# A three-layer graph attention stack on one core: own products in the first sixteen blocks, one running maximum instead of two and a join, extremes one count tile later

## The reference

```python
h = x @ W
s, d = h @ a_src, h @ a_dst
e = leaky_relu(s[src] + d[dst], 0.2)
m = segment_max(e, dst)
ex = exp(e - m[dst])
alpha = ex / segment_sum(ex, dst)
out = segment_sum(alpha[:, None] * h[src], dst) + b
```

## Time and profile before

| | us |
|---|---|
| median of 3 runs (lowest, highest) | 688.24 (688.14, 689.72) |
| the profiled execution | 687.7 |
| its span | 686.0 |
| busy: PE / DVE / ACT / POOL | 587.9 / 639.8 / 484.7 / 459.6 |

### The profile page before, as it was taken

The page is one execution under the profiler, slowest core; times in us unless marked ns, Lnnn a source line. Parts: engine busy times, 40 slices in busy tenths (PEclk is TensorE's granted clock), DMA queues, the critical chain, the costliest instruction groups (busy, mean ns, idle before and its releaser), DMA issues.

```text
span 686.0 us, 13824 instructions
## 1 busy us (share of the span) xinstructions
PE 587.9 (86%) x5571; PEld 570.1 (83%) x5571; DVE 639.8 (93%) x911; ACT 484.7 (71%) x719; POOL 459.6 (67%) x448
## 2 busy tenths in 40 slices
PE   1728845989869899999999979999989989999995
PEld 1628744988769899989999979899989979999994
DVE  3999979999999989999987999999998899999994
ACT  0416543655969787887765878989886698898891
POOL 5579103589908656675954775858598688697883
PEclk9959977899999899999999999999999999999998
DMA  2410002000000000000100100000010010110001
GB/s 69 119 56 2 1 9 38 1 2 1 20 1 1 20 1 20 1 1 9 20 20 1 27 1 20 1 19 2 8 20 20 1 27 3 37 29 11 20 1 42
DMA packets 22325, 12.07 MB, mean 18 GB/s; under 512 B 12393, under 2 KB 20055, under 8 KB 22255
## 3 DMA queue, kind: packets, MB, share of 16 engines
q1 hardware_dynamic: 21455, 9.85, 6.2%
q0 software_dynamic: 800, 1.26, 0.6%
HBM read 9.47 MB, written 1.64 MB: 16 GB/s over the span
## 4 chain that ended last, share of the span: by engine, by line
DVE 52%; PE 28%; issue 8%; DMA 6%; POOL 4%; ACT 1%; POOLq 0%; DVEq 0%; SPq 0%
PE ps L1813 21%; DVE scratch L951 21%; DVE ps L1067 16%; DVE scratch L1149 5%; DMA xr<-in_x 3%; POOL scratch L751 2%; DVE ps L1069 2%; DVE ps L1079 1%; PE ps L1866 1%; PE ps L1821 1%; DMA gathered<-ext_lines 1%; PE ps L1844 1%; DVE scratch L1067 1%; DMA gathered<-in_edges,start_i 1%; DMA ext_lines<-ext 1%
## 5 line engine op out<-in xcount | busy, mean ns | idle before, releaser
L1813 PE MATMUL ps<-hB,scratch 125*125 125x129 f32 x3450 | 404.7, 276 | 21.3 <-DVE scratch L1149 17.8
L1813 PEld LDWEIGHTS ps<-hB,scratch 125*125 125x125 f32 x3450 | 390.7, 189 | 28.6 <-DVE scratch L1149 23.0
L751 POOL TENSOR_TENSOR scratch<-scratch,C 125x625 f32<-125x625 f32 x239 | 304.1, 1283 | 124.1 <-ACT scratch L1569 122.1
L1067 DVE SCALAR_TENSOR_TENSOR ps<-C,a_unit,ps 125x625 f32<-125x625 fp8e3 x330 | 275.5, 867 | 2.3
L1567 ACT ACTIVATE scratch<-gathered,r_neg 125x625 f32<-125x625 f32 x219 | 176.6, 806 | 18.7 <-PE ps L1813 17.5
L1569 ACT ACTIVATE scratch<-scratch,r_src 125x625 f32<-125x625 f32 x219 | 179.0, 817 | 7.1
L1452 ACT ACTIVATE C<-ps 125x1000 fp8e3<-125x1000 f32 x80 | 78.0, 1000 | 78.5 <-PE ps L1780 78.3
L1780 PE MATMUL ps<-scratch 128*128 128x125 bf16 x1250 | 90.3, 235 | 40.0 <-DVE scratch L951 38.1
L1780 PEld LDWEIGHTS ps<-scratch 128*128 128x128 bf16 x1250 | 83.0, 105 | 46.8 <-DVE scratch L951 44.7
L1149 DVE SCALAR_TENSOR_TENSOR scratch<-ps,r_src,C 125x625 f32<-125x625 f32 x121 | 104.2, 861 | 4.2 <-PE ps L1803 4.1
L951 DVE TENSOR_TENSOR scratch<-key_lo,ps 128x4096 bf16<-128x4096 bf16 (+3 forms) x41 | 89.8, 2190 | 0.0
(11 more groups left out here) (195 smaller groups left out, 451.5 us busy)
## 6 DMA issues: line engine op xcount, KB each, us to landing
gathered<-g_lines SPq DMA_DIRECT2D x15, 305.2 KB
xr<-in_x SPq DMA_DIRECT2D x1, 1562.5 KB
out<-xr SPq DMA_DIRECT2D x4, 312.5 KB
edge_sb<-in_edges SPq DMA_DIRECT2D x1, 805.7 KB
gathered<-ext_lines SPq DMA_DIRECT2D x5, 122.1 KB
w<-in_W SPq DMA_DIRECT2D x2, 128.0 KB
out<-xr SPq DMA_DIRECT2D x1, 187.5 KB
out<-xr SPq DMA_DIRECT2D x1, 125.0 KB
```

Of the source, the lines that this page charges most:

```text
L751: g.tensor_tensor(slot[s], slot[s], C5[:, q % NC, s, :], ALU.mult).then_inc(pool_done, 1)
L1067: v.scalar_tensor_tensor(dest, counts, unit[:, s:s + 1], top, ALU.min, ALU.max).then_inc(S.top_done, 1)
L1813: last = mm(ps[0:P, acc_at(t):acc_at(t) + HW], A[:, P * t:P * (t + 1)], feat, start=opens and t in (0, 3), stop=closes, skip_group_check=True)
```

## The change

- One accumulator `TOP0` for all tops of a chunk; the join goes, and every top waits for the top before it. Top 24 writes `top_a`.
- Other tables of own products. The number per chunk stays (4, 9, 7, 11, then 12, 10, 10, 10, 10, 12, 9, 9, 9, 9). Chunks 6 to 9 have 0, 1, 2, 4, 6, 8, 10, 12, 14 and 16 (20 and 24 have become 6 and 12), chunks 11 to 14 have 1, 2, 4, 6, 8, 10, 12, 14 and 16 in the same manner. Chunks 5 and 10 keep theirs.
- The next row of G comes two blocks behind the last own product: after block 21, 19 and 19 in chunks 1 to 3, after 18 in chunks 6 to 8 and 11 to 13. Chunks 4 and 9 keep 22, chunks 5 and 10 keep 23. Its wait for the tops goes.
- The extremes are taken at count tile 15 instead of 14 and reduced two tiles later (17) instead of one (15). Chunk 0's blocks then lie in tiles 22 to 35.

```diff
-        OWN = ((), (15, 18, 20, 22), (1, 4, 7, 10, 13, 15, 18, 20, 22), (1, 5, 9, 13, 16, 19, 22), (0, 2, 4, 7, 10, 12, 14, 16, 18, 20, 22))
+        OWN = ((), (13, 15, 17, 19), (0, 2, 4, 7, 9, 11, 13, 15, 17), (1, 3, 5, 8, 11, 14, 17), (0, 2, 4, 6, 8, 10, 12, 14, 15, 16, 18))
...
-        EXT_AT = FEAT_AT[-1] + 2
-        OVER_AT = EXT_AT + 1
+        EXT_AT = FEAT_AT[-1] + 3
+        OVER_AT = EXT_AT + 2
...
-        MORE = (0, 6, 12, 18, 22)
+        INNER = ((0, 1, 2, 4, 6, 8, 10, 12, 14, 16), (1, 2, 4, 6, 8, 10, 12, 14, 16))
...
-            if q < NC:
-                return ODD
             if turn(q):
                 return tuple(sorted(ODD + TURN_MORE))
-            return tuple(sorted(ODD + MORE[(1 if q < 2 * NC else 0):]))
+            return tuple(s for s in range(T) if s not in INNER[q // NC - 1])
...
         def rows_at(q):
-            return 23 if turn(q) else 22
+            return 22 if q % NC == NC - 1 else min(23, max(s for s in range(T) if s not in POOL_OF[q]) + 2)
...
-                odd = in_odd(s, q if S is F else None)
-                at_ = TOP1 if odd else TOP0
-                top = ps[0:P, at_:at_ + CD]
-                same = [k for k in range(s) if in_odd(k, q if S is F else None) == odd]
-                if same:
-                    dve.wait_ge(S.top_done, n + same[-1] + 1)
-                elif q:
+                n = q * T + s
+                top = ps[0:P, TOP0:TOP0 + CD]
+                if n:
                     dve.wait_ge(S.top_done, n)
...
-            def join_tops(S, q):
-                dve.wait_ge(S.top_done, q * (T + 1) + T)
-                v.tensor_tensor(top_a, top_a, ps[0:P, TOP0:TOP0 + CD], ALU.max).then_inc(S.top_done, 1)
...
                 for t in range(CT):
-                    if t == CT - 1 and q > 1:
-                        pe.wait_ge(F.top_done, tops_before_rows(q))
```

More of the change, by code:

```diff
@@ L441, in post_at @@
             return TURN[L] if turn(q) else BEFORE_LAST[L] if q % NC == NC - 1 and L < 2 else USUAL[L]
-        def in_odd(k, q=None):
-            if q in (1, 2):
-                return k % 2 == 1 and not any(at_ == AFTER and (c, k) == (q, k_) for at_, c, k_ in FIRST_TOPS[q])
-            return k >= AHEAD and k % 2 == 1
-        LAST_ODD = max(k for k in range(T) if in_odd(k))
-        def tops_before_rows(q):
-            if q in (2, 3):
-                c, k = min((c, k) for at_, c, k in FIRST_TOPS[q - 1] if at_ == AFTER)
-                return c * (T + 1) + k
-            return q * (T + 1) if q > 1 else 0
         def top_at(q, k):
@@ L459, in top_at @@
             return (k - AHEAD) * (T - 3) // (T - 1 - AHEAD)
-        def join_at(q):
-            return top_at(q, T - 1) if turn(q) else top_at(q, T - 1) + 1
         def rows_at(q):
-            return 23 if turn(q) else 22
+            return 22 if q % NC == NC - 1 else min(23, max(s for s in range(T) if s not in POOL_OF[q]) + 2)
         def pool_no(q, s):
@@ L1053, in top_step @@
                 counts = C5[:, q % NC, s, :]
-                n = q * (T + 1)
-                odd = in_odd(s, q if S is F else None)
-                at_ = TOP1 if odd else TOP0
-                top = ps[0:P, at_:at_ + CD]
-                same = [k for k in range(s) if in_odd(k, q if S is F else None) == odd]
-                if same:
-                    dve.wait_ge(S.top_done, n + same[-1] + 1)
-                elif q:
+                n = q * T + s
+                top = ps[0:P, TOP0:TOP0 + CD]
+                if n:
                     dve.wait_ge(S.top_done, n)
-                if s == LAST_ODD and q:
+                if s == T - 1 and q:
                     dve.wait_ge(S.top_T, q)
-                dest = top_a if s == LAST_ODD else top
-                if same:
+                dest = top_a if s == T - 1 else top
+                if s:
                     v.scalar_tensor_tensor(dest, counts, unit[:, s:s + 1], top, ALU.min, ALU.max).then_inc(S.top_done, 1)
@@ L1162, in first_tops @@
                         next_top(c, k)
-                        if k == T - 1:
-                            join_tops(F, c)
             def chunk(q):
@@ L1178, in chunk @@
                                 next_top(q, k)
-                        if s == join_at(q):
-                            join_tops(F, q)
                     if q:
@@ L1371, in careful_chunk @@
                     top_step(K, a_unit[0], q, i)
-                join_tops(K, q)
                 for part in range(3):
@@ L1784, in top_transpose @@
             def top_transpose(S, q):
-                pe.wait_ge(S.top_done, (q + 1) * (T + 1))
+                pe.wait_ge(S.top_done, (q + 1) * T)
                 if q:
```

## The result

The changed kernel takes 703.85 us in the median (703.76 to 704.38), the kernel before beside it 688.19. The ratio is 1.0225, with a 95% interval of 1.0211 to 1.024: by it 15.5 us slower; the spans of the two profiles are 702.0 and 686.0. The forecast was 694.8 with a range of 687.5 to 700. The sign was right, the size was not.

The account below looks back on a forecast made before the run. VectorE and TensorE were taken to bound the kernel in turns: their loop in chunks 6 to 9, VectorE's sum in chunks 11 to 14. Terms summed to +6.5, 694.2 profiled, 694.8 us median; range 687.5 to 700.

Parts of the forecast that it names:

- Count stage, -3.4: Count stage: later extremes remove VectorE's 3.39 us wait for them, -3.4 us, bounds -3.4 and 0.
- The price of a chained pair and of a join: VectorE's tops: one following a top of the same accumulator costs 0.13 us more; a join costs 0.72 us.
- The rival of a free chain: VectorE's tops: chained tops cost nothing extra, so dropping joins gains and the time is 677.3 us; chance 0.13.
- Start of chunk 1, +3.5: Start of chunk 1: block 13's product now comes first, delaying block 15 and the reduction; +3.5 us, bounds 0 and 6.
- Chunks 2 to 4, +0.3: Chunks 2 to 4: more chained pairs, fewer joins, denser products, TensorE waiting elsewhere about as much; +0.3 us, bounds -0.5 and +2.
- Chunks 6 to 8, +4.8: Chunks 6 to 8: the TensorE-VectorE loop grows by 1.4 us and ScalarE adds 0.2, 1.6 a period; +4.8 us.
- Chunk 9, 0: Chunk 9: the same +1.4 us at block 14, offset by less waiting for GpSimd; 0, bounds -0.5 and +1.5.
- Chunks 11 to 13, +1.0: Chunks 11 to 14, three periods: VectorE's added work costs +0.3 us each; +1.0 us, bounds -1.5 and +3.
- VectorE's sum: Chunks 11 to 14: VectorE's total work, issued without a gap, sets the period; +1.04 - 0.72 = +0.3 us each.
- The end, +0.9: End of chunk 14: GpSimd's last block becomes 24, adding 1.28 less 0.4; +0.9 us, bounds 0 and +2.6.
- The row of G: Next row of G sooner, without its wait: VectorE waited only at the start of chunks 5 and 10; 0 us.
- The rival of eight GpSimd blocks in a row: Blocks 17 to 24, all GpSimd's: TensorE waits 1 us more in chunks 6 to 14, 7 more, 701.8; chance 0.15.

Follow-up runs that it names:

- e1: Kernel before with only the extremes taken one tile later and reduced two tiles later; 685.66 us, ratio 0.9953.
- e2: Kernel before with only one accumulator and no join, old product tables kept, row of G not waiting for the tops; 693.71 us, ratio 1.0073.
- e9: Kernel before with block 22 in place of block 8 as VectorE's product in chunks 6 to 9; 691.81 us, ratio 1.0034.
- e11: Kernel before with VectorE's blocks 6 and 12 for 20 and 24 in chunks 6 to 9 and 11 to 14; 698.32 us, ratio 1.0144.
- e5: Kernel before with the new tables of VectorE's own products in chunks 1 to 4 alone; 693.5 us, ratio 1.0076.
- e7: Kernel before with block 6 in place of block 20 for VectorE in chunks 6 to 9 and 11 to 14; 696.31 us, ratio 1.011.
- e8: Kernel before with block 12 in place of block 24 for VectorE in chunks 6 to 9 and 11 to 14; 690.31 us, ratio 1.0021.
- e4: Changed kernel with the next row of G back at block 22 or 23; 705.33 us, ratio 1.0229 to the kernel before.

## Why the prediction was right or wrong

The forecast was +6.5 on the profiled execution, the profile has +16.0. The terms that were too small are those of chunks 2 to 4 (by 2.3 us), the end (2.1), the start of chunk 1 (1.75), chunks 11 to 13 (1.3) and chunk 9 (1.1).

- **Count stage, -3.4.** Right: -3.6 in the table, -3.2 alone (e1).
- **The price of a chained pair and of a join.** Right: 0.912 against 0.775, and e2 costs 5.0 where the price gives 5.5. The rival of a free chain falls. So does the rule of the Trainium skill ("VectorE: DVE Perf Modes", section "The DRAIN you can't avoid") as applied to this pattern, where every top needs the one before.
- **Start of chunk 1, +3.5.** The mechanism was right (block 13's product ahead of two blocks and the transpose), the term too small: +5.25 in the table, 4.4 for the chunk's table of products alone. What failed is "I take the stretch at 1.2 GHz as falling half into it: -1.7". The idle time of 7.28 us ended with the clock already at the low level, and blocks 13 and 14 and the transpose ran wholly at it, 2.8 us more on the way to the reduction. In the kernel before the low clock cost about 1.1 at the reduction in chunk 2 (32.0 us from one reduction to the next, 30.9 in e9 and e11, which have no fall). That 3.5 + 1.7 comes to the measured 5.25 is in part luck: the stage differs by 1.1 between profiles of the same code.
- **Chunks 2 to 4, +0.3.** Wrong: +2.6, above the bound of 2. "VectorE's products come denser; TensorE waits at other blocks by about as much" left both costs out. The chain costs 2.1 here (e2), the tables 1.7 (e5). In the changed kernel +1.4 lie between the reductions in chunks 3 and 4, where e2 has +1.6 and e5 nothing, and +1.1 between those in chunks 4 and 5, where e5 has +1.15 and e2 nothing; there TensorE waits 0.57 for GpSimd and 0.26 for ScalarE.
- **Chunks 6 to 8, +4.8.** Right in sum, +5.2, but in part by luck, as two errors cancel. In e7 block 6's product costs 0.8 a period and ScalarE's late copy up to 0.9 ("1.2 us of that are slack", "+0.2"). Block 12's product, forecast at +0.5 with the chained tops beside it, costs 0.25 alone (e8) and nothing on top of block 6 (e11).
- **Chunk 9, 0.** Wrong: +1.1, inside the bound of 1.5 that was given. TensorE's wait of 0.92 for GpSimd at block 15 goes, as was said, but a new one of 1.24 for GpSimd comes ahead of the last two blocks. e7 has +1.03 here by other waits: 0.46 for GpSimd at block 15, 0.39 for the copy, 0.57 for GpSimd at the end.
- **Chunks 11 to 13, +1.0.** VectorE's sum was the right limit for two of the three periods and was sized too small: the periods are 29.77 and 29.75 with no idle time at the reduction, 0.6 more than before and not 0.3; e2 has 0.5. The third, 30.29, holds 0.48 of idle time at its reduction, behind the wait for block 24. So some 1.8 of the 2.3 are VectorE's sum and 0.5 GpSimd. The limit that GpSimd sets stands close under the other: without a chain, e11 has 29.71, 29.72 and 30.25, and each of its reductions waits. The two do not add.
- **The end, +0.9.** Wrong: +3.0. "One more is 1.28, less 0.4" counted block 24 (e8: +1.0) and forgot block 20, whose product GpSimd has to fit in between its additions to the output (e7: +1.96).
- **The row of G.** Right, no effect on the time (e4). But with the new tables and the row at its old place VectorE would wait for it; the change puts that idle time at the reduction.

The rival of eight GpSimd blocks in a row was priced at 7 us, with a chance of 0.15 ("1 us more in each of the chunks 6 to 14 but the turn", which are eight chunks and not seven). Its 701.8 lies nearer to the 703.85 than the forecast, but not by its own working: GpSimd's waits show in chunk 9, at the end and, with 0.5, in chunk 14's reduction, and they make less than half of the missing 9.5 us. The direction was seen, and it belonged into the forecast in part and not beside it.

The terms of chunk 9, of the end and the copy in chunks 6 to 8 share one error: the moved product was costed where it arrives and not where it leaves. Block 20's work went to ScalarE ahead of the copy and to GpSimd ahead of the end. ScalarE was busy for 484.7 of the 686.0 us and GpSimd for 459.6, but neither had time to spare at these places.

Left open: why VectorE's sum in chunks 11 to 13 rises by 0.6 where the eight chained pairs less a join that were counted give 0.3; and which product of the new tables brings the waits in chunk 4.
